# A two-branch transformer layer on one core: first-batch weight handling, early transposes, and key stacks filled from SyncE

## The reference, cut to what matters

```python
xn = layernorm(x)                        # no gain, no bias
xh = xn[:, :, :128]                      # branch 0 works on half of the columns
xs = holt(xn)[:, :, :128]                # branch 1: exponential smoothing along the tokens
x1 = layernorm(xh + mha(xh, ...)) * g1 + be1      # 8 heads of 16, softmax over 2048 keys
x2 = layernorm(xs + mha(xs, ...)) * g2 + be2
y  = concat(x1, x2)
f  = relu(y @ w_ff1.T + b_ff1) @ w_ff2.T + b_ff2  # 256 -> 1024 -> 256, "the first network"
ff = layernorm(y + f) * g_ff + be_ff
s  = relu(xn @ W1 + b1) @ W2 + b2                 # "the second network"
out = x + ff + s
```

## Time and profile before

| | |
|---|---|
| median of 3 runs | 2804.95 us (2801.73 to 2811.61) |
| the profiled execution | 2801.63 us |
| its span | 2800.0 us |
| TensorE busy (matmul) | 2600.6 us, 93% |
| ScalarE busy | 2206.4 us, 79% |
| VectorE busy | 1546.7 us, 55% |
| GpSimd busy | 427.1 us, 15% |
| mean share of the 16 DMA engines | 7.3% from SyncE's queue, 5.7% from GpSimd's |
| mean granted TensorE clock | 0.976 of full speed |

### The profile page before, as it was taken

How to read it: one execution, slowest core, us unless ns; L and a number is a source line. 1 busy time by engine, 2 the same in 40 slices (tenths; PEclk the granted TensorE clock), 3 DMA queues, 4 the chain that set the end, 5 groups by cost and what they waited for, 6 DMA issues and landing times.

```text
span 2800.0 us, 53558 instructions
## 1 busy us (share of the span) xinstructions
PE 2600.6 (93%) x19305; PEld 959.3 (34%) x19305; DVE 1546.7 (55%) x3226; ACT 2206.4 (79%) x2409; POOL 427.1 (15%) x404
## 2 busy tenths in 40 slices
PE   2899999998889999999898999999988999999985
PEld 1322222224532222223463222222355222222253
DVE  7554555554764454555375455555558444554566
ACT  1489999993469999998347999999555999999932
POOL 3501000002520100000351010000054010000142
PEclk9999999999999999999899999999999999999998
DMA  3511010002220101000412011000031010100001
GB/s 137 101 39 32 9 32 9 9 5 81 55 77 9 32 9 32 14 8 5 116 31 62 9 32 28 20 9 5 20 101 46 24 32 9 32 9 9 5 27 39
DMA packets 50528, 95.00 MB, mean 34 GB/s; under 512 B 8768, under 2 KB 33344, under 8 KB 49872
## 3 DMA queue, kind: packets, MB, share of 16 engines
q1 hardware_dynamic: 39504, 65.70, 7.3%
q0 software_dynamic: 10752, 25.71, 5.7%
HBM read 57.23 MB, written 34.08 MB: 33 GB/s over the span
## 4 chain that ended last, share of the span: by engine, by line
PE 79%; DVE 7%; POOL 5%; issue 4%; ACT 2%; DMA 1%; DVEq 0%; POOLq 0%; ACTq 0%; SPq 0%
PE slot L1184 35%; PE slot L1160 19%; PE slot L1031 7%; PE slot L1045 6%; POOL p_sb L490 3%; PE slot L1224 3%; PE slot L1016 2%; PE slot L1085 2%; ACT p_sb L584 2%; PE slot L1115 1%; PE slot L1214 1%; POOL k_st L446 1%; POOL q_st L446 1%; DVE stats L652 1%; PE slot L1113 1%
## 5 line engine op out<-in xcount | busy, mean ns | idle before, releaser
L584 ACT ACTIVATE p_sb<-slot 128x1024 f32<-128x1024 f32 x2048 | 1938.2, 1030 | 160.8 <-PE slot L1160 150.0
L1184 PE MATMUL slot<-p_sb,v_sb 128*17 128x512 f32 x8192 | 1082.0, 600 | 12.6 <-ACT p_sb L584 10.7
L1160 PE MATMUL slot<-q_st,k_st 50*128 50x512 f16 x4096 | 625.2, 384 | 19.7 <-issue 10.7
L1160 PEld LDWEIGHTS slot<-q_st,k_st 50*128 50x128 f16 x4096 | 133.8, 94 | 894.7 <-ACT p_sb L584 598.9
L719 DVE TENSOR_SCALAR hid_one<-slot,b_grown 128x256 f32<-128x256 f32 x256 | 123.9, 484 | 297.5 <-PE slot L1031 294.0
L731 DVE SCALAR_TENSOR_TENSOR second<-slot,second 128x256 f32<-128x256 f32 x64 | 27.2, 425 | 401.3 <-PE slot L1045 401.3
L1184 PEld LDWEIGHTS slot<-p_sb,v_sb 128*17 128x17 f32 x8192 | 136.1, 95 | 323.8 <-ACT p_sb L584 196.2
L446 POOL DMA_DIRECT2D k_st<-part_dram x96 | 48.0, 507 | 1188.9 <-PE slot L1184 958.6
L685 DVE RECIPROCAL rden<-den 128x256 f32<-128x256 f32 x128 | 224.4, 1753 | 7.5
L1031 PE MATMUL slot<-xt_parts,w_parts 128*128 128x256 f16 x1536 | 213.0, 275 | 4.5 <-DVE hid_one L719 4.5
L1045 PE MATMUL slot<-w_parts,hid_parts 128*128 128x256 f16 x1536 | 212.1, 274 | 0.0
(11 more groups left out here) (112 smaller groups left out, 2020.3 us busy)
## 6 DMA issues: line engine op xcount, KB each, us to landing
part_dram<-p_sb SPq DMA_DIRECT2D x16, 1024.0 KB, 4.0
k_st<-part_dram POOLq DMA_DIRECT2D x96, 128.0 KB, 5.8
q_st<-part_dram POOLq DMA_DIRECT2D x96, 128.0 KB, 8.1
xn<-x SPq DMA_DIRECT2D x16, 512.0 KB, 6.5
second<-x SPq DMA_DIRECT2D x32, 256.0 KB, 3.5
ffn_dram<-second SPq DMA_DIRECT2D x32, 256.0 KB, 2.0
area<-ffn_dram SPq DMA_DIRECT2D x16, 512.0 KB, 4.9
out<-area SPq DMA_DIRECT2D x16, 512.0 KB, 3.3
```

The costliest lines, as they stand in the source:

```text
L584: act.activation(p_sb[:, n % 4, :], slot[n % 3][:, :], ACT.Exp, scale=0.25 / GROW ** 2).then_inc(exp_done, 1)
L1160: mm = pe.matmul(slot[at % 3][:, k * CHUNK:(k + 1) * CHUNK], k_st[rows_, pair, kt * P:(kt + 1) * P], q_st[rows_, pair, c_ * CHUNK:(c_ + 1) ...
L1184: mm = pe.matmul(o_bank[ROW * j:ROW * j + DK + 1, :], v_sb[:, a, kt, GH * g + j, :], p_sb[:, n % 4, (j % 2) * CHUNK:(j % 2 + 1) * CHUNK], ...
```

## The change

In the first batch:

- The second network's weights: ScalarE makes the f16 part of `w_raw` (times 64) ahead of its prologue, VectorE the low part in one instruction behind its prologue; the same for the first network, ScalarE behind its prologue and VectorE right after the other. GpSimd's `split` is gone. GpSimd waits for the low part of `w_raw` before it fills `q_st`, TensorE before attention.
- The check of the second network's weights leaves the place ahead of attention, and TensorE's column sum with it (`ones_w` and `squares` go too). W1 is now checked element by element. All checks of weights and biases are in the last batch: four small ones in unit 1, four of 2048 columns in units 5, 7, 9 and 11.
- X_GROW is 8 in place of 16.

In every batch:

- TensorE's transposes wait per group of the layer norm (`normed`), not for all four groups and the first state of the smoothing.
- The 12 fills of `k_st` for branch 0 are issued by SyncE, between the maxima of branch 0 and the spills of branch 1, and counted by semaphores of their own (`k_first_in`). GpSimd keeps the 16 fills of `q_st` there, and all 28 of branch 1.

```diff
-X_GROW, Y_GROW, W_GROW = 16.0, 4.0, 64.0
+X_GROW, Y_GROW, W_GROW = 8.0, 4.0, 64.0
...
+            def fill(eng, a, g, stack, parts, which, landed):
+                pairs = slice(GH // 2 * g, GH // 2 * (g + 1))
+                for half in range(2):
+                    for r, part in enumerate(parts):
+                        src = part_dram[a, which, part, DK * GH * g:DK * GH * (g + 1), :]\
+                            .rearrange("(n h d) s -> h d n s", h=2, d=DK)[half]
+                        at = HALF * half + DK * r
+                        eng.dma_start(stack[at:at + DK, pairs, :], src).then_inc(landed[g], 16)
+                    if which:
+                        at = HALF * half + STACK
+                        eng.dma_start(stack[at:at + 2, pairs, :], m_dram[a, :, GH * g + half:GH * (g + 1):2, :])\
+                            .then_inc(landed[g], 16)
...
 # SyncE, prologue(b), behind the maxima of branch a
+                        if a == 0:
+                            hold(sp, k_out, 16 * (br + 1) + 16)
+                            for g in range(GROUPS):
+                                fill(sp, 0, g, k_st, K_PART, 0, k_first_in)
...
 # GpSimd
                 def prologue(b):
                     spilled(2 * b)
+                    if isinstance(b, int):
+                        pool.wait_ge(w_split, 2)
                     for g in range(GROUPS):
-                        fill(0, g, k_st, K_PART, 0)
-                        fill(0, g, q_st, Q_PART, 1)
+                        fill(pool, 0, g, q_st, Q_PART, 1, stack_in)
...
                     prologue(b)
-                    split(wf_raw, wf_parts, wf_in, wf_split)
-                    pool.tensor_scalar(bf_grown[:, :], c("b_ff1"), Y_GROW * W_GROW, None, ALU.mult).then_inc(wf_split, 1)
-                    pool.wait_ge(wf_split, 4)
+                    pool.wait_ge(wf_split, 2)
                     residual(b)
...
-                split(w_raw, w_parts, raw_in, w_split)
                 pool.wait_ge(consts_in, 16)
...
 # ScalarE
                 def first(b):
+                    act.wait_ge(raw_in, 16)
+                    act.activation(w_parts[:, 0], w_raw, ACT.Identity, scale=W_GROW).then_inc(w_split, 1)
                     prologue(b)
+                    act.wait_ge(wf_in, 16)
+                    act.activation(wf_parts[:, 0], wf_raw, ACT.Identity, scale=W_GROW).then_inc(wf_split, 1)
...
 # VectorE
                     normalise([xn[:, t, :] for t in range(CT * q, CT * (q + 1))])
+                    dve.sem_inc(normed, 1)
...
                 prologue(0)
-                weights_fine()
+                for raw, parts, done in ((w_raw, w_parts, w_split), (wf_raw, wf_parts, wf_split)):
+                    dve.wait_ge(done, 1)
+                    dve.scalar_tensor_tensor(parts[:, 1], raw, W_GROW, parts[:, 0], ALU.mult, ALU.subtract).then_inc(done, 1)
+                dve.wait_ge(bias_grown, 2)
...
-                            if not next_norm and n in NORM_UNITS[:3]:
-                                first_weights_fine(NORM_UNITS.index(n))
+                            if not next_norm and n == 1:
+                                weights_fine(((0, c("b1"), B1_LIMIT), (1, c("b_ff1"), BF_LIMIT),
+                                              (2, c("gamma"), GAMMA_LIMIT), (3, c("beta"), BETA_LIMIT)))
+                            if not next_norm and n in NORM_UNITS:
+                                i_ = NORM_UNITS.index(n)
+                                lo = i_ % 2 * 2 * FF
+                                weights_fine(((4 + i_, (w_parts, wf_parts)[i_ // 2][:, 0, lo:lo + 2 * FF],
+                                               (W1_LIMIT, W2_LIMIT, WF1_LIMIT, W2_LIMIT)[i_]),))
...
 # TensorE
-                    pe.wait_ge(xn_ready, b + 1)
                     for j in range(4):
+                        pe.wait_ge(normed, CHUNKS * b + 2 * (j % 2) + 2)
...
-                            hold(pe, stack_in[g], 16 * LOADS * (2 * b + a + 1))
+                            hold(pe, stack_in[g], 16 * ((K_LOADS + 2 * Q_LOADS) * b + (Q_LOADS, K_LOADS + 2 * Q_LOADS)[a]))
+                            if a == 0:
+                                hold(pe, k_first_in[g], 16 * K_LOADS * (b + 1))
...
                     prologue(b)
-                    weights_fine()
+                    pe.wait_ge(w_split, 2)
```

More of the change, by code:

```diff
@@ L318, in fast_programs @@
             stack_in = [sem(f"stack_in_{g}") for g in range(GROUPS)]
+            k_first_in = [sem(f"k_first_in_{g}") for g in range(GROUPS)]
             scores_made = sem("scores_made")
@@ L436, in pool_program @@
             def pool_program(pool):
-                def fill(a, g, stack, parts, which):
-                    pairs = slice(GH // 2 * g, GH // 2 * (g + 1))
-                    for half in range(2):
-                        for r, part in enumerate(parts):
-                            src = part_dram[a, which, part, DK * GH * g:DK * GH * (g + 1), :]\
-                                .rearrange("(n h d) s -> h d n s", h=2, d=DK)[half]
-                            at = HALF * half + DK * r
-                            pool.dma_start(stack[at:at + DK, pairs, :], src).then_inc(stack_in[g], 16)
-                        if which:
-                            at = HALF * half + STACK
-                            pool.dma_start(stack[at:at + 2, pairs, :], m_dram[a, :, GH * g + half:GH * (g + 1):2, :])\
-                                .then_inc(stack_in[g], 16)
                 def spilled(br):
@@ L473, in refill @@
                         hold(pool, pv_done, TILES * (UNITS2 * b + CHUNKS * (g + 1)) + 2)
-                        fill(1, g, k_st, K_PART, 0)
-                        fill(1, g, q_st, Q_PART, 1)
+                        fill(pool, 1, g, k_st, K_PART, 0, stack_in)
+                        fill(pool, 1, g, q_st, Q_PART, 1, stack_in)
                 def first_y(b, cc):
@@ L513, in last @@
                     nets(b)
-                def split(raw, parts, arrived, done):
-                    pool.wait_ge(arrived, 16)
-                    pool.tensor_scalar(raw, raw, W_GROW, None, ALU.mult).then_inc(done, 1)
-                    pool.wait_ge(done, 1)
-                    pool.tensor_copy(parts[:, 0], raw).then_inc(done, 1)
-                    pool.wait_ge(done, 2)
-                    pool.tensor_tensor(parts[:, 1], raw, parts[:, 0], ALU.subtract).then_inc(done, 1)
                 pool.sem_inc(y_ready, 1)
@@ L858, in prologue, with weights_fine @@
                             turn(1)
-                def first_weights_fine(n):
-                    at = B * UNITS2 + 3
+                def weights_fine(tests):
                     flat = area[:, 0:2 * FF]
-                    if n == 0:
-                        dve.wait_ge(wf_split, 4)
-                        tests = (("bf", c("b_ff1"), BF_LIMIT), ("gamma", c("gamma"), GAMMA_LIMIT), ("beta", c("beta"), BETA_LIMIT))
-                    else:
-                        lo = (n - 1) * 2 * FF
-                        tests = ((f"w{n}", wf_parts[:, 0, lo:lo + 2 * FF], (WF1_LIMIT, W2_LIMIT)[n - 1]),)
-                    for i, (name, tile, limit) in enumerate(tests):
-                        col = at + (i if n == 0 else 2 + n)
+                    for i, tile, limit in tests:
+                        col = B * UNITS2 + i
                         part = flat[:, 0:tile.shape[-1]]
@@ L1195, in transpose_y @@
                         pe.wait_ge(ff_read, n)
[L1196 removed]
+                    pe.wait_ge(wf_split, 2)
                     for k in range(2):
@@ L1226, in nets @@
                         mm.then_inc(net_done, 1)
-                def weights_fine():
-                    pe.wait_ge(sums_read, 1)
-                    for k in range(2):
-                        for f in range(2):
-                            mm = pe.matmul(slot[2][:, k * CHUNK:(k + 1) * CHUNK], ones_w[:, :],
-                                           squares[:, f * FF + k * CHUNK:f * FF + (k + 1) * CHUNK], start=(f == 0), stop=(f == 1))
-                    mm.then_inc(sums_made, 1)
-                    pe.wait_ge(sums_read, 2)
                 def first(b):
-                    pe.wait_ge(v_ones_made, 3)
+                    pe.wait_ge(v_ones_made, 2)
                     prologue(b)
-                    weights_fine()
+                    pe.wait_ge(w_split, 2)
                 def middle(b):
```

41 lines of the change are left out of this document (6 added, 35 removed).

## The result

The changed kernel takes 2820.76 us (median of 5 runs, 2820.68 to 2821.73) against 2804.34 us for the kernel before (5 runs). The ratio is 1.0056, with a 95% interval of 1.0042 to 1.0071: slower by 0.56%, more than the 0.3% that the prediction took for what a measurement here can tell, and above its range of 2776 to 2808. The profiled execution took 2820.71 us with a span of 2819.2, so the sum of the differences has to come to +19.2 us of span, where the prediction had -12.0.

A forecast was written before the change was run, and what follows sets the result against it. TensorE, busy for 93% of the span, was taken as the bound, with idle time at the start and between batches. From 2801.6 us: -22.9 - 7.1 - 8.6 + 26 + 0.6 = -12.0, so 2789.6 (2793.0 on the median); range 2776 to 2808.

The forecast's parts named there:

- start, to the first scores: Kernel start to the first batch's first scores: they start at 96.0 in place of 118.85, 22.9 us earlier.
- first batch's attention: First batch, first unit: weight checks and GpSimd's split leave, saving 7.1 us, or between 4 and 8.
- delay at three boundaries: Between batches: spills queued behind SyncE's k fills hold the first network activation, 8.0, 9.2 and 8.8 us, together +26.
- stall, and the rest of the boundaries: Second boundary: GpSimd's stall after 128 fills moves to the third batch's refill and is hidden, -8.6 us or nothing.
- other three attentions (added waits): Attention: six added waits of TensorE per batch, +0.6 us in all, from nothing to 2.
- the spills' delay eats it all: ScalarE's hold at each boundary: decides from 12.7 us a boundary; up to +11.4 us, 2816, slower; chance 0.2.
- bound of 45: Three boundaries: if both queues share 0.147 equally, k is done at 707, spills at 714: 45 us in all.
- The layer norm: Kernel start: without GpSimd's pass, the third group's scalings take 1.38 us; key projection starts at 33.4, 25.3 us earlier.
- The bounds, 92 and 100.3: First scores: 4 us behind the last q fill issue (92), or the 12.28 us it took before (100.3).
- The last batch's checks: Last batch: two more checks of 2048 columns cost nothing; 12 us of VectorE if their cover were gone.

The follow-up runs named there:

- e3: The changed kernel, with GpSimd's q fills of branch 0 waiting, from the second batch on, until SyncE's k fills have landed: 2792.61 us, ratio 0.9944.
- e4: The kernel before, with only the twelve k fills of branch 0 issued by SyncE ahead of the spills, and their semaphores: 2846.12 us, ratio 1.0141.
- e8: e1 with TensorE's transposes waiting again for all four groups of the layer norm and the smoothing's first state: 2772.89 us, ratio 0.9882.
- e6: e1 with the low part of the second network's weights made early, in VectorE's idle gap inside the first prologue: 2768.04 us, ratio 0.9864.
- e7: e6 with group 0's six k fills ahead of branch 1's spills in the first batch alone: 2760.17 us, ratio 0.9837.
- e2: The changed kernel, with branch 0's k fills issued by GpSimd again, in the first batch ahead of its wait for the weights: 2777.66 us, ratio 0.9897.
- e1: The changed kernel, with SyncE's twelve k fills moved behind branch 1's spills and maxima: 2772.31 us, ratio 0.9874.
- e9: e1, but in the first batch alone SyncE's k fills stand ahead of branch 1's spills as in the changed kernel: 2766.18 us, ratio 0.9861.
- e5: A kernel of only transfers, not the reference's work: narrow fills from SyncE, GpSimd or both, and wide transfers; twelve narrow fills take 14 us from either queue.

## Why the prediction was wrong

Term by term, forecast and measured in the span of the two profiled executions:

| term | forecast | measured |
|---|---|---|
| start, to the first scores | -22.9 | -19.65 |
| first batch's attention | -7.1 | -6.0 (577.38 to 571.36) |
| delay at three boundaries | +26 | +55.3 (17.7 + 19.3 + 18.3) |
| stall, and the rest of the boundaries | -8.6 | -7.6 |
| other three attentions (added waits) | +0.6 | +1.9 |
| tail | 0 | -4.7 |
| sum | -12.0 | +19.2 |

**The step that failed** is the delay at the boundaries, and in it one sentence: "GpSimd's q fills run beside them in the other queue; I let SyncE's queue keep its rate, since with both backlogged hardware got 0.66 MB and software 0.12". The place, the waiting engine and the missing cover were right: `yt_hi` waits for the spill at every boundary. What was wrong is the rate. In the earlier trace rows SyncE's queue held spills over 128 partitions. In the changed kernel it holds fills of 16, as GpSimd's does, and then both halve: 0.93 MB from SyncE and 0.80 from GpSimd in 667 to 681 us, 0.125 MB/us together. The twelve k fills are through near 681, 19 us after the first issue, where the prediction had 10.7. The spills then take 9.5 more beside the rest of the q fills, where it had 6.4 and a margin of 2.3, and 0.6 lie ahead of the issue: 0.6 + 19 + 9.5 = 29.1, beside 29.7 measured. e3 shows the term without the sharing: k in 13.8 us and the spills 5.7 later. So of the 8.3 us by which k was too late, 5.2 are the sharing, and 3.1 are the rate and the start of lone fills, which were set too favourably. That e3 comes out at the forecast 20 is luck, since its spills run without company. e4 shows the edit alone: +39.5 us.

The mean granted clock of the first boundary is 0.89, against 0.95 before, but its matmuls take 90.7 us against 91.0: the clock is low while TensorE waits, and the longer wait costs no more than itself.

**The rival that came true** is "the spills' delay eats it all", and the measured 55.3 lie beyond even its bound of 45, so the bound was no bound. It put the spills at 0.33 MB/us behind shared fills (714); with GpSimd's last q fills beside them they took 9.5 us and not 6.4, three times over. The argument against the rival was the earlier trace rows, which shows another case.

**The start.** The layer norm (-24.65 against -25.3) was right, by the mechanism named: with no GpSimd pass beside them, VectorE's four scalings take 1.38 us (e8 has the parts). VectorE's low part started at 80.65 and not 79.3, and the last maxima of group 0's q fills, issued at 89.10, landed 9.57 us later in the chain, where 7 were allowed. These 1.1 to 1.4 and 2.6 us, less 0.5 that the scores start sooner behind the landing, are the 3.2. The bounds, 92 and 100.3, held. e6 and e7 show that the wait of GpSimd for the low part mattered little as long as the fills behind it were in the wrong order: alone, its removal gave 3.5 us, with k of group 0 ahead of the spills another 11.3.

**The first batch.** -6.0 against -7.1, within the bounds. The cause was not tested by itself. The traces agree with the one named: after 24 exps the two kernels stand alike (23.8 and 24.2 us behind the first), after 32 the kernel before is 6.3 us later, and in its 130 to 160 us TensorE waits for VectorE's `hid_one`,

```profile
L1031 PE MATMUL slot<-xt_parts,w_parts 128*128 128x256 f16 x48 | 7.5, 297 | 4.5 <-DVE hid_one L719 4.5
```

where the changed kernel's same 48 matmuls wait for nothing in 110 to 140 us.

**The stall.** It moved as forecast, by the count of fills: in the timeline of GpSimd of the changed kernel it stands in the third batch's refill, after 3 times 16 and 2 times 28 fills and 24 more, which is 128.

```profile
1755.12 1.47 POOL L368 DMA_DIRECT2D q_st<-part_dram  x3 [2.48 <-issue]
```

But it is 2.48 us there, 1.88 in e2 and 2.38 to 2.48 in all the others, against 10.20 in the one profile of before, so its price can't be read off its place. The price of 8.6 was also more than a wait. Behind the stall of before, ScalarE waits 8.12 us for GpSimd and TensorE 5.57 for ScalarE, and then the granted clock is at half for 6.8 us. The first and second boundary of before and that stretch (from:to, us, TensorE busy (matmuls), clock, DMA share, GB/s):

```profile
696.23:801.95 105.72, 91.01 (x609) 0.95 0.31 64
1372.27:1485.33 113.06, 96.03 (x608) 0.91 0.29 58
1391.70:1398.50 6.80, 5.98 (x17) 0.50 0.37 48
```

So 5.0 of the 7.3 us between the two boundaries are the same matmuls taking longer. In the second boundary of the changed kernel they take 93.2 us. There the delay grew by 19.3 and the stretch by 11.9: 7.4 us came back, 2.8 of them in the matmuls, and 8.6 were forecast. e2 has the stall at the old place and a second boundary of 105.4 us. So the 7.4 go with the stall's length, which I can't explain, and the move alone is not shown to have saved them.

**The tail.** Nothing was forecast. The row of the last instruction in the chain of the changed kernel, and then in that of the kernel before:

```profile
2812.61 0.14 DVE again L974
```

```profile
2787.49 0.14 DVE again L999
```

From there to the end of the span it is 2819.16 - 2812.75 = 6.4 us now and 2800.0 - 2787.63 = 12.4 before. It is 13.6 in e2, 6.4 in e1, e3 and e6 to e9, and 6.7 in e4. So the short end goes with k fills issued from SyncE, the long one with GpSimd's; why stays open. The 7.2 us between e2 and e1 are the whole of the 6.9 by which e2's tail is longer.

**The last batch's checks.** That attention took 1.1 us more (517.14 to 518.24) where nothing was forecast. One execution can't tell so little: with the same checks it takes 517.1 us in e3 and e9 and 519.0 in e1 and e6 to e8. No cost is shown.

## What to carry to other kernels

Read a transfer rate from the profile together with the shape at the head of each queue: a rate seen for transfers over 128 partitions says nothing for a queue filled with 16-partition ones, and two narrow streams share one rate whichever engines issue them. Before moving DMA issues into another queue, write down what stands behind them there and who waits for it: here the same twelve fills per boundary cost some 50 us more in the whole ahead of two spills than behind them. Last, order by first reader across both queues: the first group's k fills ahead of the spills and of the other group's was worth more (11.3 us) than starting the q fills ten us earlier (3.5). And where a number comes true, as e3's 20 us, still compare it term by term: two errors of 3 us can cancel.

## What the runs showed of the hardware

- Fills of 16 partitions by 8 KB move 0.11 to 0.16 MB/us in all, from SyncE, GpSimd or both: 0.112 and 0.109 over twelve with their start and landing, 0.130 over 24 (e5), 0.132 alone in a boundary (e3), 0.157 in the first batch of the changed kernel. The same bytes over 128 partitions move 0.258. The Trainium skill, "SBUF — State Buffer" (Door 1), gives 104 GB/s to partitions 0 to 15 for one transfer of 1 MiB, which is near the twelve with their ends and too low for a queue that is kept full.
- A wide transfer beside a narrow one takes 84.8% of the engines' time against 16.0%; two narrow ones 53.6% against 51.3%, once both are moving. A narrow queue that starts behind the backlog of the other moved nothing for 5 us or more (e1, e6).
- GpSimd's queue pauses once, after 128 of its transfers, for 10.20 us (before), 2.38 to 2.48 or 1.88 us (e2). What sets the length was not found.
- The granted clock is at half for 6.8 us behind a wait of 5.57 us in the second boundary of before; the boundary's matmuls take 96.0 us against 91.0 in the first.
- The span runs on for 6.4 to 6.7 us or for 12.4 to 13.6 us after the last instruction, by which engine issues the k fills. Not explained.
